# Expert layers of a small transformer moved into a third instruction stream that borrows PSUM banks

## The chip, the cores and the metric

The kernel runs on one core of a Trainium2 chip. The metric is the device time of one execution in microseconds, from runs of the whole kernel; one more execution was recorded by the hardware profiler, and all rows below are from it. Engines: TensorE (PE, with its weight loads as PEld), VectorE (DVE), ScalarE (ACT), GpSimd (POOL) and SyncE (SP), which here issues the DMAs.

## What is computed

Eight independent batch elements (batches 0 to 7 for short) of 256 tokens by 128 features pass through two layers, each with modulated layer norms (scale, shift and a gate from a small condition vector).

```python
# layer 0, attention: an indexer picks 96 keys per query (64 local ones and the best of the others)
I = einsum('bths,h->bts', relu(q_i @ k_i.T), idx_w); idx = top_k(I, 96)
scores = (q_c . k_c[idx] + q_r . key_r[idx]) * scale;  out = softmax(scores) @ v[idx] @ W_out
# layer 0, FFN: two layers of windowed attention (8 heads, window 64) and a gated GELU network
# layer 1, attention: 16 heads of size 8, full softmax over 256 tokens
# layer 1, FFN: mixture of experts, computed for all 16 experts and one shared one
score = sigmoid(h @ gate_w.T);  top 8 of 16, weights normalised, times 2.826
y = down_0(silu(gate_0(h)) * up_0(h)) + sum_e weight_e * down_e(silu(gate_e(h)) * up_e(h))
```

Everything is float32 but the gather of keys, which multiplies one-hot matrices in bf16 with keys split into three bf16 parts.

## The kernel before, in words

**Two streams.** Elements 0, 2, 4, 6 form stream 0 and elements 1, 3, 5, 7 stream 1. Each stream has its own arena in SBUF (`mem[s]`, whose parts are used again by one stage after the other) and four of the eight PSUM banks (`banks(s)`: bank 4s + i). For each engine there is a generator per stream (`tensor_stream` line 519, `scalar_stream` 1158, `vector_stream` 1544, `pool_stream` 2073, `sync_stream` 446) that issues the instructions of its four rounds and yields between steps. `turns` (line 125) interleaves the two generators of an engine by a string written out in `STEPS_IN_TURN` (line 97): each character is a number of steps, and the streams alternate. So the order of every engine is fixed in the program, and the engines meet through semaphores (`Signals`: `at(name, n)` is the value to wait for, `one(name)` the increment).

**One round of a stream:** front (transposes of the input at line 811, layer norm, projections 826 to 840, index scores 849, top-32 search on VectorE 1777 to 1785, indices written to DRAM and read back to all partitions 455 to 468, one-hot compares 1798, gather matmuls 557), sparse attention, two windowed layers (wqkv 728 and 733, scores 671, turns 616, values 687, FFN 1002 to 1018), the 16-head attention (1033 to 1101), and the experts (1109 to 1137).

**The experts before** stand at the end of each stream's round. TensorE computes the router product, the transposes of x and the gate row into bank 3 (1113 to 1116), and gate and up of the shared expert. Then for four groups of four experts: `expert_downs` of the group before (780s, matmul at 795) overwrites the banks of its own ups, `expert_gates` (matmul at 772) writes banks 0 and 1, `expert_ups` (780) waits for the last sums (1133, 1135), because it writes banks 2 and 3 again. ScalarE applies silu (1524) and scales two of the four products (1512, summed by GpSimd at 2187 and 2191). VectorE first adds the other two products (`expert_sum`, 1636) and then multiplies silu by up for the next group (2032). GpSimd adds the halves, applies the gate row and the residual (2195, 2199, 2202), and SP stores the result (490). The next round's first transpose waits for the last silu (809), its variance matmul for the last sum (819), and its second index projection for the last scaled product (838). The tiles `moe_g`, `moe_h`, `y`, `y2`, `x_res`, `gate_row`, `tmp` and `routes` lie in the stream's arena.

**Filler.** `keep_busy` (527) issues matmuls into a bank whose content nobody reads, as many as the next character of `BUSY` says (line 103 on), ahead of waits.

**Tables.** `table` (1149) loads ScalarE's function table when the next function, in the order of issue, needs another one than the last: one for Ln and Exp (line 1153), one each for Gelu and Silu (line 1155).

Of the kernel before, what the change touches and what calls it, by code (L numbers as in the profile page):

```python
# [49 lines left out]
def shape_constants():  # L50
# [47 lines left out]
    "pe": ("822112244222g26437677323236617321212244113t1a3a5841528171a455a4632a372a4522362121d672a15222846222112222424411212"  # L98
            "221212212132115142113111123125531224212523272221217272643767732323661732121224411221f1c1a2a5841528171a3611281612"
            "31225151a452a1a1612413272a45252512282824272211123212222231114211515251511122212515152525232222527266376773232366"  # L100
            "17321212245321z021218282112229482c1k1612413272a351a321818413272a452525122828232224141122121232431152515142115111"
            "2221251515252523222252726236855743234349141222231112312231a1c3c584632a371a5558425682c3c1816222352h672f1a28232624"
            "21121222121221111211211341134115351515335"),
    "act": ("d212437327322a9274312464634322162623338122m23338262536488223426223348327221b27223345522ef33321313343545523344421"
            "35a2235442182c5542a52464634322162623338142i22231382625364a22111282421132228252322a21334822332l42j433445351536233"
            "421134553233352j573212311234312464634322162623338142n2332222364f2a2322a21334d422322623334822332g321332g321134153"
            "53546233421134553233352l55321342b43564433328233334623152a2335822172322334882224162723353317h46223a2lf43423333445"
            "2334253a225"),
    "dve": ("t4o1b89645494c4369441444544652431e341441p361c41c571c442395117571744236134a1c5715412541444242412ju151335c35583523"
            "85d3m9213833434b4e44681331144321443652471d311441h3d1d41c591e4325416541a442a2521855174429311531553134123j1112z091"  # L110
            "51431c328335c365b833256411351d4d4c78341444544652431e341441v37164591444111k25218551747111645216551744293115414541"
# [181 lines left out]
def program(nc, A, out, idx_scratch, score_scratch):  # L293
    ctx = ExitStack()
    with ctx:
# [124 lines left out]
        def cols(k):  # L420
            return slice(P * k, P * k + P)
# [1867 lines left out]
```

## Time and profile before

| what | us |
|---|---|
| timed runs, median of 3 (lowest, highest) | 1416.68 (1406.8, 1420.68) |
| the profiled execution's own time | 1413.97 |
| its span, first to last instruction | 1412.1 |
| mean granted TensorE clock over the span | 0.968 |
| TensorE busy | 1221.4 |
| VectorE busy | 905.8 |
| ScalarE busy | 868.7 |
| GpSimd busy | 362.2 |

Busy time is the union of an engine's instructions. A matmul's end is modelled and matmuls are pipelined, so a busy TensorE is not TensorE at its peak. Idle time in a row is that just before the group's instructions on the same engine, with what ended it behind the arrow; "issue" means that nothing the profile shows was waited for.

### The profile page before, as it was taken

The numbers are of one execution on the slowest core, as the hardware profiler recorded it, in microseconds if no ns is written. First come the engines' busy times: TensorE is split into PE (matmuls) and PEld (weight loads), VectorE is DVE, ScalarE is ACT, GpSimd is POOL, SyncE is SP. The second block draws the span as 40 slices with busy tenths as digits, with TensorE's granted clock in tenths as the row PEclk, the third lists the DMA queues.
The fourth block names the chain that finished last, engine by engine and source line by source line (L and its number), as shares of the span: only waits on it lengthen the run. The fifth ranks groups of instructions, "written<-read, shape, count | busy, mean of one in ns | idle before, by whom it ended". The sixth has DMA issues, their size and how long they took to land.

```text
span 1412.1 us, 29992 instructions
## 1 busy us (share of the span) xinstructions
PE 1221.4 (86%) x11446; PEld 850.2 (60%) x11446; DVE 905.8 (64%) x2920; ACT 868.7 (62%) x2237; POOL 362.2 (26%) x580
## 2 busy tenths in 40 slices
PE   7879988878988988888999799788899799898787
PEld 5546555646864655565776566556677465565466
DVE  3966676553685776765376666776546767767643
ACT  3426677538652766755775477774576467776563
POOL 0710343100281132311154022231015402422103
PEclk9889999989998998999999999999999999999999
DMA  8121000000013000000011200000001210000000
GB/s 299 49 80 23 2 1 1 1 5 5 5 59 81 15 2 1 1 1 5 5 50 29 77 4 1 1 2 1 5 9 50 74 30 2 1 1 1 1 1 8
DMA packets 31791, 34.84 MB, mean 25 GB/s; under 512 B 19168, under 2 KB 23712, under 8 KB 31136
## 3 DMA queue, kind: packets, MB, share of 16 engines
q1 hardware_dynamic: 31648, 32.92, 7.8%
q8 instruction: 91, 1.49, 0.4%
q14 instruction: 52, 0.43, 0.1%
HBM read 25.46 MB, written 7.44 MB: 23 GB/s over the span
## 4 chain that ended last, share of the span: by engine, by line
PE 53%; ACT 19%; DVE 16%; issue 4%; DMA 3%; POOL 2%; SPq 1%; DVEq 0%; POOLq 0%; ACTq 0%
ACT arena L1415 5%; PE ps L795 4%; ACT arena L1164 4%; PE ps L557 4%; PE ps L780 3%; PE ps L772 3%; PE ps L728 3%; ACT arena L1468 2%; DVE small L1958 2%; PE ps L1069 2%; DMA idxb<-idx_scratch 2%; PE ps L657 2%; PE ps L530 2%; PE ps L1052 2%; PE ps L1088 2%
## 5 line engine op out<-in xcount | busy, mean ns | idle before, releaser
L1164 ACT ACTIVATE arena<-ps 128x512 f32<-128x512 f32 (+7 forms) x560 | 258.7, 485 | 235.0 <-PE ps L580 31.3
L2106 POOL TENSOR_TENSOR arena<-arena 128x512 f32<-128x512 f32 x64 | 80.9, 1275 | 310.0 <-DVE arena L1609 308.7
L1415 ACT ACTIVATE arena<-arena,small 128x128 f32<-128x128 f32 (+1 forms) x256 | 129.9, 511 | 2.2 <-DVE small L1895 1.9
L1584 DVE CUSTOM_DVE_ANT_0 arena<-ps,mask_w_bf 128x128 f32<-128x128 f32 (+1 forms) x256 | 67.6, 321 | 65.9 <-PE ps L671 65.6
L530 PE MATMUL ps<-mean_mat 128*128 128x256 bf16 x612 | 88.0, 287 | 15.3 <-ACT arena L1164 11.7
L1958 DVE TENSOR_REDUCE small<-ps 128x4 f32<-128x1024 f32 x64 | 75.5, 1219 | 29.3 <-PE ps L1052 29.0
L1362 ACT ACTIVATE arena<-arena,small 128x224 f32<-128x224 f32 (+1 forms) x128 | 56.6, 448 | 49.7 <-DVE small L1843 49.7
L1468 ACT ACTIVATE arena<-ps 128x512 f32<-128x512 f32 x128 | 66.6, 602 | 31.3 <-PE ps L1088 31.1
L530 PEld LDWEIGHTS ps<-mean_mat 128*128 128x128 bf16 x612 | 58.8, 102 | 41.5 <-issue 16.6
L2032 DVE TENSOR_TENSOR arena<-arena,ps 128x512 f32<-128x512 f32 x64 | 42.9, 686 | 60.9 <-ACT arena L1524 47.8
L1819 DVE TENSOR_TENSOR gath<-ps,rank_tab 96x512 f32<-96x512 f32 x96 | 62.4, 680 | 29.5 <-PE ps L565 15.3
L795 PEld LDWEIGHTS ps<-w_experts,arena 128*128 128x128 f32 x544 | 64.3, 191 | 26.8 <-issue 15.2
L795 PE MATMUL ps<-w_experts,arena 128*128 128x128 f32 x544 | 69.1, 279 | 12.5 <-DVE arena L2032 7.8
L557 PE MATMUL ps<-hot_ring,arena 128*96 128x512 bf16 x192 | 56.5, 438 | 25.8 <-DVE gath L1819 18.1
L1572 DVE TENSOR_TENSOR arena<-arena,small 128x512 f32<-128x512 f32 x96 | 69.3, 722 | 3.1
L728 PE MATMUL ps<-w_wqkv,arena 128*128 128x512 f32 x128 | 64.6, 643 | 2.1 <-DVE arena L1562 2.1
L2191 POOL TENSOR_TENSOR arena<-arena 128x256 f32<-128x256 f32 x32 | 24.0, 751 | 165.1 <-ACT arena L1512 163.4
L780 PE MATMUL ps<-arena,w_experts 128*128 128x256 f32 x272 | 65.5, 381 | 0.0
L616 PE MATMUL ps<-packed,arena 128*128 128x128 f32 x384 | 61.8, 284 | 4.2 <-DVE arena L1575 2.3
L772 PE MATMUL ps<-arena,w_experts 128*128 128x256 f32 x272 | 65.3, 379 | 0.0
L1512 ACT ACTIVATE arena<-ps,arena 128x128 f32<-128x128 f32 x128 | 36.7, 373 | 35.7 <-PE ps L795 35.1
L1584 DVE CUSTOM_DVE_ANT_0 arena<-ps,mask_a_bf,small 128x192 f32<-128x192 f32 (+1 forms) x128 | 41.6, 380 | 25.9 <-PE ps L603 25.5
(288 smaller groups left out, 2934.4 us busy)
## 6 DMA issues: line engine op xcount, KB each, us to landing
idxb<-idx_scratch SPq DMA_DIRECT2D x24, 512.0 KB, 5.2
score_scratch<-arena SPq DMA_DIRECT2D x96, 64.0 KB, 1.7
w_experts<-in_experts SPq DMA_DIRECT2D x3, 1088.0 KB, 17.1
w_wqkv<-in_wqkv SPq DMA_DIRECT2D x1, 1536.0 KB, 9.2
arena<-score_scratch SPq DMA_DIRECT2D x96, 16.0 KB, 2.1
arena<-in_x SPq DMA_DIRECT2D x8, 128.0 KB, 2.2
out_x<-arena SPq DMA_DIRECT2D x8, 128.0 KB, 1.8
packed<-in_packed SPq DMA_DIRECT2D x2, 503.0 KB, 4.0
```

Source lines behind the costliest of these rows:

```text
L530: mm(to, still[:, 0:P], still, start=True, stop=True)
L557: last = mm(bank[g % 2][0:GF, :], m.kv_part[i][:, 0, :], hot[n][:, part], start=(i == 0), stop=(n < 2 and i == 2))
L728: mm(bank[2 * k + j], m.sh[:, cols(k)], wqkv[:, l, 512 * j:512 * j + 512], start=True, stop=True)\
L772: last = mm(bank[j // 2][:, L * (j % 2):L * (j % 2) + L], experts[:, 0, e, :], m.hT, start=True, stop=True)
L780: last = mm(to[:, L * (j % 2):L * (j % 2) + L], experts[:, 1, e, :], m.hT, start=True, stop=True)
L795: last = mm(bank[2 + j // 2][:, 256 * (j % 2) + P * k:256 * (j % 2) + P * k + P], m.moe_h[:, L * j + P * k:L * j + P * k + P], experts[:, ...
L1164: return act.activation(dst, src, ACT.Copy)
L1415: ins = act.activation(probs, probs, ACT.Exp, bias=nb[s][:, i, h:h + 1], scale=cqs[s][:, T, hh_:hh_ + 1], accum_out=ls[s][:, i, h:h + 1])
L1468: act.activation(m.PT1[v][:, q, :, :].rearrange("p j n -> p (j n)"), bank[q], ACT.Exp, scale=SCALE_1)\
L1584: ins = dve.tensor_tensor_reduce(masked[:, h, 0:n], bank[h % 2][:, n * (h // 2):n * (h // 2) + n], mask, 1.0, least(h), ALU.add, ALU.max, ...
L1958: st.mark(dve.tensor_reduce(to, src, AX.X, ALU.max))
L2106: ins = pool.tensor_tensor(own, own, turned, ALU.add)
```

## The change

The experts leave the streams' rounds and become a third generator on each engine (`expert_tensor`, `expert_scalar`, `expert_vector`, `expert_pool`, `expert_sync`), which runs through all eight elements in order. Its tiles move to one set of their own (`LateViews`, 4096 floats per partition), shared by all elements; only `routes` is there twice. The last layer norm of a round writes `late.hT`.

It has no banks of its own: each of the 18 products of an element goes to a bank named by the string `LENT`, taken from the main streams. `Loans.borrow` waits until the last readers of the owner's content are done, and `Loans.claim`, now called in front of every first write of a main stream, waits for the return of a bank that was lent. Gates, ups and downs of a group have banks of their own; downs overwrite the ups' banks as before. TensorE's order in a group becomes gates of the next group, downs of this one, ups of the next. VectorE's products of a group come before the sums of the group before.

All turn strings are new (they now name the stream of each turn), so are the counts of filler: 612 matmuls before, 516 after, and none in front of the downs. The two waits for the output's store in the front (479, 2148) go. The DMA scratch is cut to 512.

```diff
 def turns(engine):
-    s = 0
-    for n in STEPS_IN_TURN[engine]:
-        yield from [s] * int(n, 36)
-        s = (s + 1) % NS
+    runs = STEPS_IN_TURN[engine]
+    for s, n in zip(runs[::2], runs[1::2]):
+        yield from [int(s)] * int(n, 36)
...
+class Loans:
+    def __init__(self):
+        self.emptied, self.returned = {}, {}
+    def claim(self, pe, bank, *emptied):
+        if bank in self.returned:
+            pe.wait_ge(*self.returned.pop(bank))
+        self.emptied[bank] = emptied
+    def borrow(self, pe, bank, returned):
+        for wait in self.emptied.pop(bank, ()):
+            pe.wait_ge(*wait)
+        if bank in self.returned:
+            pe.wait_ge(*self.returned.pop(bank))
+        self.returned[bank] = returned
...
+        def before_in_experts(s, r):
+            return (1 - s, r) if s else ((1 - s, r - 1) if r else None)
...
             def ln_var(n):
                 yield
+                claim([2], ("ln_rstd", n + 1))
                 keep_busy(bank[2][:, 0:L])
...
-                if r > 0:
-                    pe.wait_ge(*at("e_silu", 0))
+                claim([0], ("xT_copied", 1))
                 for k in range(NT):
                     last = pe.transpose(bank[0][:, cols(k)], m.x_tok[:, k, :], ident[:, :])
...
+        def expert_tensor(pe):
...
+                for i in range(1, 6):
+                    if i < 5:
+                        for j in range(2):
+                            yield
+                            bank = borrowed(4 * i - 2 + j, "e_silu", 2 * i + j)
+                            for h in range(2):
+                                last = mm(bank[:, L * h:L * h + L], experts[:, 0, 4 * i - 3 + 2 * j + h, :], late.hT, ...)
+                            last.then_inc(*one("e_gate"))
+                    yield
+                    pe.wait_ge(*at("e_hidden", 2 * i - 1))
+                    for j in range(1 if i == 1 else 2):
...
+                        last.then_inc(*one("e_down"))
+                    if i < 5:
+                        ups = []
+                        for j in range(2):
+                            yield
+                            name, count = ("e_sum", i + 1) if j == 0 else ("e_tmp", i)
+                            ups.append(borrowed(4 * i + j, name, count))
...
+                            last.then_inc(*one("e_up"))
...
# scalar: the copy of the next input waits until the router has read xT; in the third stream silu comes ahead of the scaling
                 act.wait_ge(*at("x_turned", 1))
+                if r > 0:
+                    act.wait_ge(*at("route_mm", 0))
                 copy(m.xT, bank[0][:, 0:L]).then_inc(*one("xT_copied"))
...
# vector, third stream
                 for i in range(1, 6):
-                    yield from expert_sum(i - 1)
                     if i < 5:
...
                             dve.wait_ge(*at("e_silu", 2 * i + j))
+                            dve.wait_ge(*at("e_down", 2 * i - 1))
                             dve.wait_ge(*at("e_up", 2 * i + j))
-                            dve.wait_ge(*at("e_down", 2 * i - 1))
...
+                    yield from expert_sum(i - 1)
...
+            streams = [tensor_stream(pe, s) for s in range(NS)] + [expert_tensor(pe)]
...
-    nc = bacc.Bacc("TRN2", target_bir_lowering=False, num_devices=1)
+    nc = bacc.Bacc("TRN2", target_bir_lowering=False, num_devices=1, dynamic_dma_scratch_size=512)
```

In the third stream an element's first writes into the shared tiles wait for the element before: `late.hT` for its last up products, silu for its last hidden product, VectorE's first hidden product for its last downs, `x_res` for its last sum, `y` for its store.

## Rows read from the trace of the kernel before

**Rows 1.** The page: span and busy time of each engine.

```profile
span 1412.1 us, 29992 instructions
...
PE 1221.4 (86%) x11446; PEld 850.2 (60%) x11446; DVE 905.8 (64%) x2920; ACT 868.7 (62%) x2237; POOL 362.2 (26%) x580
```

**Rows 2.** Groups by line: busy, mean ns of one, idle before and its releasers.

```profile
L530 PE MATMUL ps<-mean_mat 128*128 128x256 bf16 x612 | 88.0, 287 | 15.3 <-ACT arena L1164 11.7 <-DVE arena L1594 2.6 <-DVE arena L1636 1.1
L795 PE MATMUL ps<-w_experts,arena 128*128 128x128 f32 x544 | 69.1, 279 | 12.5 <-DVE arena L2032 7.8 <-DVE arena L2020 4.3
L780 PE MATMUL ps<-arena,w_experts 128*128 128x256 f32 x272 | 65.5, 381 | 0.0
L772 PE MATMUL ps<-arena,w_experts 128*128 128x256 f32 x272 | 65.3, 379 | 0.0
L795 PEld LDWEIGHTS ps<-w_experts,arena 128*128 128x128 f32 x544 | 64.3, 191 | 26.8 <-issue 15.2 <-ACT arena L1500 7.0 <-ACT arena L1524 3.9
...
L557 PE MATMUL ps<-hot_ring,arena 128*96 128x512 bf16 x192 | 56.5, 438 | 25.8 <-DVE gath L1819 18.1 <-DVE hot_ring L1798 7.0 <-ACT arena L1164 0.6
```

**Rows 3.** Line 1493, the router, in two windows: durations in ns, first and last start.

```profile
L1493 ACT ACTIVATE arena<-ps x2: 198/207/216, 327.5 to 356.1; 128x32 f32<-128x32 f32 x2
...
L1493 ACT ACTIVATE arena<-ps x2: 198/213/228, 1351.1 to 1366.2; 128x32 f32<-128x32 f32 x2
```

**Rows 4.** Line 811, first transposes of elements 2 and 3, 345 to 420 us.

```profile
L811 PE MATMUL ps<-packed,arena x4: 272/272/273, 365.8 to 394.8; 128*128 128x128 f32 x4
```

**Rows 5.** Busy time by stretch, with experts and fronts (first of three, and the sum).

```profile
core 0: us, PE busy (x) PEld busy (x) DVE busy (x) ACT busy (x) POOL busy (x), PEclk, DMA share, GB/s
327.00:480.00 153.00, 137.59 (x1381) 101.52 (x1379) 99.05 (x353) 96.64 (x245) 46.47 (x68) 0.97 0.14 38
...
sum 463.00, PE 419.62 PEld 306.58 DVE 287.90 ACT 294.45 POOL 135.44; mean PE 139.87 PEld 102.19 DVE 95.97 ACT 98.15 POOL 45.15
```

**Rows 6.** The same for the three stretches between them.

```profile
480.00:668.00 188.00, 158.43 (x1395) 103.55 (x1391) 126.17 (x363) 117.71 (x307) 44.92 (x76) 0.96 0.01 2
...
1165.00:1350.00 185.00, 158.24 (x1483) 103.90 (x1480) 123.05 (x362) 124.74 (x326) 45.14 (x76) 1.00 0.00 1
sum 560.00, PE 475.78 PEld 314.76 DVE 378.76 ACT 363.64 POOL 134.78; mean PE 158.59 PEld 104.92 DVE 126.25 ACT 121.21 POOL 44.93
```

**Rows 7.** Filler (line 530) alone in both sets of stretches: the two sums.

```profile
sum 463.00, PE 17.39; mean PE 5.80
...
sum 560.00, PE 42.66; mean PE 14.22
```

**Rows 8.** Busy time of three windows of 50 us, columns as in rows 5.

```profile
100.00:150.00 50.00, 47.93 (x789) 31.54 (x788) 32.62 (x120) 30.54 (x98) 4.39 (x5) 0.97 0.10 22
1050.00:1100.00 50.00, 46.98 (x323) 36.36 (x323) 36.44 (x140) 35.60 (x84) 22.83 (x37) 1.00 0.11 36
1350.00:1400.00 50.00, 48.27 (x307) 41.96 (x307) 25.88 (x78) 28.78 (x66) 7.78 (x11) 1.00 0.01 1
```

**Rows 9.** Filler (line 530) alone in the first two of them; the third has none.

```profile
100.00:150.00 50.00, 0.78 (x4) 0.97 0.10 22
1050.00:1100.00 50.00, 1.15 (x9) 1.00 0.11 36
```

**Rows 10.** Chain that ended last, 1350 to 1412: start, us, what.

```profile
1369.49 0.68 PE ps L795 x4
1370.18 1.73 PE ps L772 x8
...
1389.35 1.78 PE ps L795 x16
...
1401.71 0.70 DVE arena L2032
```

**Rows 11.** Groups by line: VectorE's sums, and ScalarE's loads of Gelu's and Silu's tables.

```profile
L1155 ACT ACT_TABLE_LOAD x40 | 51.3, 1283 | 0.7
...
L1636 DVE SCALAR_TENSOR_TENSOR arena<-ps,arena 128x128 f32<-128x128 f32 x128 | 39.0, 346 | 23.7 <-PE ps L795 21.8
```

**Rows 12.** Groups by line: the weight loads of the windowed values.

```profile
L687 PEld LDWEIGHTS ps<-arena 128*64 128x64 f32 x512 | 27.3, 137 | 38.9 <-issue 29.3 <-ACT arena L1164 9.5
```

More of the change, by code:

```diff
@@ L104 @@
[L104 to L108, printed above, removed]
@@ L511, in _ @@
                 sp.dma_start(dst, src).then_inc(sig("late_loaded"), 16)
-            streams = [sync_stream(sp, s) for s in range(NS)]
+            streams = [sync_stream(sp, s) for s in range(NS)] + [expert_sync(sp)]
             for s in turns("sp"):
@@ L530, in keep_busy, with claim @@
                     mm(to, still[:, 0:P], still, start=True, stop=True)
+            def claim(used, *emptied):
+                for i in used:
+                    loans.claim(pe, 4 * s + i, *(at(name, n) for name, n in emptied))
             def ln_center(n, src):
@@ L914, in tensor_stream @@
                 yield
+                claim(range(4), ("x_updated", 1))
                 keep_busy(bank[1][:, 0:L])
@@ L1041, in tensor_stream @@
                     yield
+                    claim(range(4), ("x_neg", v + 1))
                     if v == 0:
@@ L1108, in tensor_stream, with borrowed @@
                 yield from ln_var(5)
+        def expert_tensor(pe):
+            mm = pe.matmul
+            signals = [Signals(sig, s) for s in range(NS)]
+            for b in range(B):
+                s, of = b % NS, signals[b % NS]
+                of.r = b // NS
+                m, at, one = mem[s], of.at, of.one
+                def borrowed(n, name, count):
+                    loans.borrow(pe, lent(b, n), at(name, count))
+                    return ps[:, lent(b, n), :]
                 yield
-                keep_busy(bank[0][:, 0:L])
+                bank = borrowed(0, "x_res", 1)
@@ new lines, in expert_tensor @@
+                    for j in range(1 if i == 1 else 2):
+                        for h in range(1 if i == 1 else 2):
+                            e = 0 if i == 1 else 4 * i - 7 + 2 * j + h
+                            for k in range(NT):
+                                first = L * (2 * j + h) + P * k
+                                last = mm(ups[j][:, L * h + P * k:L * h + P * k + P], late.moe_h[:, first:first + P],
+                                          experts[:, 2, e, :], start=True, stop=True)
+                        last.then_inc(*one("e_down"))
@@ new lines, in expert_tensor @@
+                    if i < 5:
+                        ups = []
[3 more added lines that the diff above has]
+                            ups.append(borrowed(4 * i + j, name, count))
+                            for h in range(2):
+                                last = mm(ups[j][:, L * h:L * h + L], experts[:, 1, 4 * i - 3 + 2 * j + h, :], late.hT, start=True, stop=True)
+                            last.then_inc(*one("e_up"))
@@ L1488, in scalar_stream, with expert_scalar @@
                 yield from ln_rstd(5)
-                yield
+        def expert_scalar(act):
+            signals = [Signals(sig, s) for s in range(NS)]
+            for b in range(B):
+                s, of = b % NS, signals[b % NS]
+                of.r = b // NS
+                at, one = of.at, of.one
+                last = before_in_experts(s, of.r)
                 yield
```

369 lines of the change are left out of this document (212 added, 157 removed).

## The prediction

> **What bounds the kernel now.** I read the page's totals first [rows 1]: TensorE is busy 1221.4 of 1412.1 us, VectorE 905.8, ScalarE 868.7, GpSimd 362.2. The reader is to see one engine near its limit and three with room. The profiled execution took 1413.97 us against its span of 1412.1, 2.7 under the median of the three timed runs, 1416.68.
>
> TensorE's figure holds filler: 612 matmuls of line 530 whose output nobody reads, 88.0 us [rows 2]. So real matmul time is 1221.4 - 88.0 = 1133.4 us, 80% of the span. The rest, 278.7 us, is idle or filler, and the question is which part of it this change can reach.
>
> Then I cut the span at events that the trace places [rows 3, 4]. Batch 0 reaches its router (line 1493) at 327.5 us, but batch 2, the next one in the same arena, has its first transpose (line 811) only at 365.8, and batch 3 at 394.7 after batch 1's router at 356.1. In both streams the next batch waits for nearly the whole expert phase: its first transpose waits for the last silu (line 809). The last pair of routers comes at 1351.1 and 1366.2, three rounds later. One round of two batches is about 341 us ((1351.1 - 327.5) / 3).
>
> The tables by stretch have three stretches in which experts, the next fronts and the gathers run (327 to 480, 668 to 820, 1007 to 1165), and between them three in which only attention, FFN and the last block run. The first three sum to 463 us with TensorE busy 419.62 [rows 5]; filler in the same windows is 17.39 [rows 7]. Real work is 402.2 us, 86.9%. The other three sum to 560 us with 475.78 busy [rows 6] and 42.66 filler [rows 7]: 433.1 real, 77%. The emptier stretches are the ones that hold no expert work, and the turn strings of the changed kernel put none there: TensorE's string has passed the last expert turn of a pair by 1.25 rounds of the main streams. So the change can only refill the 463 us. Its first-order ceiling is 463 - 402.2 = 60.8 us.
>
> **The change part by part.**
>
> *Experts as a third stream.* Nothing is removed from TensorE but filler; the matmuls of lines 772, 780 and 795 return one for one (65.3 + 65.5 + 69.1 = 199.9 us in all [rows 2], 25 us a batch). What moves is when the next front may start: right after its stream's router products are written, so 327.5 instead of 365.8, some 38 us earlier in either stream. Seen as a chain the three reachable rounds could each give 38 us, which is more than TensorE can deliver; so TensorE's packing of the 463 us decides. How dense can it be? Three windows of 50 us bound it [rows 8, 9]: experts of the last pair 48.27 busy with no filler (96.5%); first-round gather and attention 47.93 - 0.78 = 94%; experts over a front 46.98 - 1.15 = 92%. I take 92%, the best that a mix of experts and a front reached: 402.2 / 0.92 = 437.2, so 25.8 us saved, some 9 a round. Low end: the share stays at 86.9%, nothing saved. High end: 96.5% gives 402.2 / 0.965 = 416.8, 46.2 saved.
>
> *The tail.* The last two batches have no front to overlap, and now share one set of work tiles, so batch 7's experts follow batch 6's. In the chain of waits of the end [rows 10] TensorE is the chain from 1369.5 to 1401.6 with no gap between expert pieces; a group of four experts costs 1.73 for gates, as much for ups of the same shape, and 1.78 for downs, 5.24 us. In the new order one group's ups (1.73) are followed by the next group's gates (1.73) and only then by its downs. The last VectorE product of a group, 0.70 us after the ups, is ready inside the gates. One batch alone therefore packs TensorE as two do now, and the end (scale by ScalarE 0.37 + 0.53, GpSimd pieces of 0.72 us) is the same. I take 0; if each of the four groups of batch 7 exposes its product once, it is 4 x 0.70 = 2.8 us; if the earlier order frees the 15.1 us between the two routers (1351.1, 1366.2) a little better, a gain of the same size.
>
> *VectorE forms the next products ahead of the last sums, and ups go to another bank.* Before, the ups of a group wait for the four sums of the last one (line 1133), 4 x 346 ns [rows 11] = 1.4 us, because they share banks 2 and 3. Now they don't. 32 groups make 44 us of latency; almost all of it lies beside the other stream's matmuls, since line 780's matmuls show 0.0 us of idle before them and line 795's 12.5 us [rows 2]. So 0 to -12.5 us; it is already inside the packing above, I add nothing.
>
> *Bank loans: added waits on TensorE.* A batch borrows 18 banks. Each borrow waits for the owner's last reader and each later claim for the loan's return: by count of the diff some 54 waits a batch in, some 20 out, 34 x 8 = 272 more. If satisfied they cost issue time. The nearest row is line 687, whose weight loads stand behind two or three waits: 29.3 us of "issue" idle over 512 loads [rows 12], 0.06 us. Upper end 272 x 0.06 = 16 us, if none hides under a running matmul; lower end 0, where the sequencer is ahead of the array, busy 86% of the span. I take 2 us. That they are not satisfied is the first rival.
>
> *ScalarE's tables.* Before there are 40 loads of Gelu's or Silu's table, 1283 ns each [rows 11], and about as many back. Silu steps are spread between the Exp and Ln steps of fronts, five silu steps a batch: at worst 5 x 8 pairs instead of the present 40 - 16 = 24 silu loads (16 are Gelu's), 16 more pairs, 41 us of ScalarE; at best fewer than now. ScalarE is busy 96.64 of 153 us in such a stretch [rows 5], so 56 us of idle hide most of it. I take 0 on the path; a load costs 1.28 where the next front's Ln waits behind it.
>
> *Filler.* The strings give 516 in place of 612, 96 x (88.0 / 612 = 0.144) = 13.8 us less of busy time in places where TensorE waits anyway: 0 on the path, up to 13.8. *Moved waits:* GpSimd's memset (line 2151) and the score read-back (line 479) no longer wait for the output's store; behind them stand small transfers of 16 KB and one memset a batch, and GpSimd is busy 26% of the span [rows 1], so I take 0. SP's queue now holds the output store as a stream of its own, and nobody waits for it but the next batch's first sum. The smaller DMA scratch moves nothing.
>
> Sum: 1414.0 - 25.8 + 2 = 1390.2. From the median of 1416.7 that would be 1392.9; I say **1391 us**.
>
> *A rule beside it.* TensorE was granted 0.97 of full speed in the first expert stretch [rows 5], which is its lower level (1.2 GHz) for some 6% of it (2 x 0.03) and 2.4 for the rest; of the stretches without experts the first had 0.96 and the last 1.00 [rows 6]. The Trainium skill (TensorE: Matmul & The Clock Gate, "HAM oscillation — how this bites in real kernels") puts the cost at half the throttled time, and says that waits between bursts cause it. By that rule denser fronts give back up to 463 x 0.06 / 2 = 14 us more, an estimate from the page's formula; the sum does without it, since part of that time is idle in which the clock costs nothing.
>
> **The rivals.**
>
> *Head-of-line waits (slower).* TensorE runs one written order. The third stream puts some 23 steps a batch, 184 in all, between steps of the main streams, and nearly all wait for ScalarE, VectorE or a loaned bank. One that comes early stops all three streams. For it: the downs' loads already wait 26.8 us and their matmuls 12.5 over 40 steps [rows 2], less 15.2 of issue 24.1 us, 0.6 us a step. Against it: gates show 0.0. At 0.14 us a step (25.8 / 184) the gain is gone; above 0.22 (25.8 + 14) it is slower by 1%. At 0.3 us a step: 55 - 26 = +29, so 1443 us.
>
> *No better packing (same).* The idle of the stretches is not lack of work but the fronts' chain: DMA of idxb, the compares, gathers; the gathers of line 557 wait 25.8 us for VectorE [rows 2]. If experts run out before these gaps, 86.9% stays: 1414 to 1417 us. That the change doesn't do what it says is the same case: loans that keep the main stream's claims waiting as long as the old order did.
>
> *Larger gain.* The fronts' start 38 us earlier and the clock's share bring 96.5%: 1414 - 46 + 2 = 1370 us. For it speaks that weight loads fill only 101.52 of 153 us [rows 5] against 41.96 of 50 in the last pair [rows 8]. [...]
>
> **How the numbers follow.** Forecast 1391 us (its own range 1378 to 1403): 0.50. Larger gain, 1370: 0.19. No better packing, 1415: 0.18. Head-of-line waits, 1443: 0.13. The bound of 1% is 14 us, about what a measurement of this kernel can tell from no change (its three runs lie 1406.8 to 1420.7). Faster by over 1%: most of the first and all of the second, 0.67. Within 1%: 0.20. Slower: 0.13. The range for 8 in 10 is 1362 to 1424: it leaves out the worst of the waits and packing beyond 96.5%.
>
> **What would show it.** First transposes (line 811) of batches 2 and 3 within some 5 us of routers 0 and 1; rounds of some 332 us between routers of one stream; TensorE's real share of the expert stretches at 92% and that between them still near 77%; the end after the last router near 43 us. Wrong if real share stays at 87%, if idle in front of the expert lines passes 50 us, if loads of Gelu's and Silu's tables exceed 55, or if the span between the stretches changes by more than 10 us: then the new order, not the third stream, made the result.

## The result and the profile after

The changed kernel takes 1403.1 us, median of 16 runs (1395.18 to 1416.66), against 1415.95 us of the kernel before, also 16 runs. The ratio is 0.9912, 95% interval 0.9889 to 0.9934: 12.8 us or 0.9% faster, where 1391 us and 1.8% were forecast. The direction was right and the gain half of the forecast. The profiled execution spans 1401.2 us against 1412.1 [rows 1].

The page of the changed kernel, span and busy time of each engine:

```profile
span 1401.2 us, 29802 instructions
...
PE 1211.0 (86%) x11350; PEld 846.4 (60%) x11350; DVE 901.3 (64%) x2920; ACT 864.8 (62%) x2231; POOL 361.8 (26%) x580
```

TensorE has 96 matmuls less, the 96 filler ones, and is busy for the same share of the span. Groups by line that answer to [rows 2] and [rows 11]; filler is line 588 now, the downs are 1219, gates 1210, ups 1229, VectorE's products 2153, its sums 2098, and the loads of Gelu's and Silu's tables 1248:

```profile
L588 PE MATMUL ps<-mean_mat 128*128 128x256 bf16 x516 | 73.0, 287 | 11.0 <-ACT arena L1257 5.1 <-DVE arena L1704 3.2 <-ACT arena L1338 2.3
L1219 PE MATMUL ps<-w_experts,late 128*128 128x128 f32 x544 | 71.5, 285 | 8.9 <-DVE late L2153 5.3 <-DVE late L2144 3.6
L1219 PEld LDWEIGHTS ps<-w_experts,late 128*128 128x128 f32 x544 | 68.2, 198 | 16.7 <-DVE late L2153 8.9 <-DVE late L2144 5.0 <-issue 1.3
L1210 PE MATMUL ps<-late,w_experts 128*128 128x256 f32 x256 | 66.1, 393 | 2.1 <-DVE small L1931 1.3 <-ACT arena L1257 0.8
L1229 PE MATMUL ps<-late,w_experts 128*128 128x256 f32 x256 | 64.0, 387 | 4.4 <-ACT late L1617 2.3 <-DVE small L1931 1.2 <-ACT arena L1411 0.9
L1248 ACT ACT_TABLE_LOAD x37 | 47.5, 1283 | 0.7
L2098 DVE SCALAR_TENSOR_TENSOR late<-ps,late 128x128 f32<-128x128 f32 x128 | 38.8, 345 | 2.0 <-PE ps L1219 0.9
```

Idle in front of the downs fell from 12.5 to 8.9 us at the matmuls and from 26.8 to 16.7 at their loads, but gates and ups, which showed 0.0, now show 2.1 and 4.4. The table loads fell from 40 to 37. And the same expert matmuls take longer: 71.5 + 66.1 + 64.0 us and 10.7 for the shared expert (lines 1201 and 1202) are 212.3, where they were 199.9 [rows 2]. Two further executions of the changed kernel give 211.9 and 211.4. The median of a gate is the same; the extra is in some of them (gates before, then gates now; duration in ns, lowest, median and highest):

```profile
L772 PE MATMUL ps<-arena,w_experts x272: 379/379/382, 327.3 to 1399.5; 128*128 128x256 f32 x136
```

```profile
L1210 PE MATMUL ps<-late,w_experts x256: 379/379/634, 327.4 to 1386.7; 128*128 128x256 f32 x128
```

The front did move. Line 853 is the first transposes of a batch (811 before, [rows 4]), line 1195 the router's matmuls; each view gives the first and the last start in its window, 300 to 400 us and, for the second router row, 1320 to 1400:

```profile
L853 PE MATMUL ps<-packed,arena x4: 272/273/273, 321.7 to 378.5; 128*128 128x128 f32 x4
L1195 PE MATMUL ps<-packed,late x8: 254/262/263, 323.9 to 380.9; 128*128 128x16 f32 x8
...
L1195 PE MATMUL ps<-packed,late x8: 254/262/263, 1328.5 to 1366.0; 128*128 128x16 f32 x8
```

Batch 2's front starts at 322 instead of 366, 2 us ahead of batch 0's router. The routers of [rows 3] are ScalarE's line; TensorE's router matmuls (line 1113 before), which compare directly with line 1195, started at 326.4 and 354.9, and at the end at 1349.7 and 1365.2. So batch 1's router comes 26 us later, at 380.6: the two streams stand 57 us apart instead of 29. Batch 6's router comes 21 us earlier, batch 7's at the same time as before within 1 us, and the end behind it takes 35 us instead of 46.

For the balance I cut both executions from stream 0's router to the end of stream 1's attention output (the products with `w_vo`, line 921 before, 970 now), so that the three stretches together hold the same work (5286 matmuls without filler before, 5273 after). First before, then after, columns as in [rows 5]; in each fence the stretches with experts:

```profile
327.00:503.00 176.00, 158.98 (x1758) 115.01 (x1758) 115.49 (x404) 111.86 (x283) 55.84 (x84) 0.97 0.12 33
668.00:856.00 188.00, 170.33 (x1869) 122.48 (x1870) 117.22 (x427) 122.05 (x311) 54.02 (x84) 0.97 0.11 31
1007.00:1187.00 180.00, 165.58 (x1835) 118.46 (x1831) 111.84 (x404) 116.79 (x292) 53.64 (x84) 0.97 0.12 32
sum 544.00, PE 494.89 PEld 355.95 DVE 344.55 ACT 350.71 POOL 163.51; mean PE 164.96 PEld 118.65 DVE 114.85 ACT 116.90 POOL 54.50
```

```profile
324.00:510.00 186.00, 167.99 (x1843) 120.52 (x1844) 119.61 (x427) 119.86 (x313) 54.77 (x84) 0.97 0.11 31
667.00:830.00 163.00, 155.45 (x1710) 112.37 (x1699) 108.41 (x384) 102.76 (x263) 47.67 (x75) 0.96 0.13 36
995.00:1168.00 173.00, 157.27 (x1777) 112.14 (x1779) 110.02 (x393) 111.69 (x283) 54.29 (x83) 1.00 0.12 34
sum 522.00, PE 480.71 PEld 345.03 DVE 338.04 ACT 334.31 POOL 156.74; mean PE 160.24 PEld 115.01 DVE 112.68 ACT 111.44 POOL 52.25
```

Filler alone in the same stretches, before and after:

```profile
sum 544.00, PE 24.71; mean PE 8.24
```

```profile
sum 522.00, PE 9.03; mean PE 3.01
```

Real work is 494.89 - 24.71 = 470.2 of 544 us before, 86.4%, and 480.71 - 9.03 = 471.7 of 522 after, 90.4%. The same work takes 22 us less. The single stretches do not hold the same work: the first has 103 matmuls more (stream 1's last block now falls into it), the second 99 and the third 17 less, so their lengths (10 us more, 25 and 7 less) say little by themselves. The real share does: 86.3 to 87.4% in the first ((158.98 - 7.15) / 176 and (167.99 - 5.51) / 186), 85.5 to 94.4% in the second, 87.6 to 89.8% in the third. The three stretches between them went from 479 to 483 us, the start from 327 to 324. Behind stream 0's last router:

```profile
1350.00:1366.00 16.00, 15.02 (x106) 11.64 (x106) 7.54 (x26) 12.43 (x23) 0.72 (x1) 1.00 0.00 1
1366.00:1412.00 46.00, 36.90 (x226) 33.27 (x224) 20.93 (x58) 18.02 (x47) 13.78 (x19) 0.96 0.02 7
```

```profile
1329.00:1366.00 37.00, 34.24 (x267) 26.87 (x267) 14.98 (x44) 27.44 (x55) 3.98 (x6) 1.00 0.00 1
1366.00:1401.00 35.00, 23.57 (x143) 20.92 (x142) 13.83 (x40) 11.72 (x29) 10.54 (x15) 0.96 0.03 8
```

62 us before, 72 after, and TensorE idle for 10.1 us of it before, for 14.2 after. So -22 + 4 - 3 + 10 = -11, the difference of the spans. But of the 10 us at the end 6 are work that now stands there, while the start holds 5.6 us less, and only 4 are new idle. To leave moved work out, take idle and filler together, and real matmul time by itself:

| us | before | changed | second execution | third |
|---|---|---|---|---|
| idle + filler, start | 80.9 | 83.5 | 80.0 | 79.2 |
| idle + filler, stretches with experts | 73.8 | 50.3 | 50.4 | 50.3 |
| idle + filler, stretches between | 113.8 | 115.0 | 114.4 | 115.1 |
| idle + filler, end | 10.1 | 14.2 | 14.1 | 14.0 |
| real matmul time | 1133.4 | 1138.0 | 1145.0 | 1142.6 |

The packing is worth 23.4 to 23.6 us in each execution. What takes it down to 11, 8 and 11 us is the end (4 us of idle) and real matmul time, which grew by 5 to 12 us, while the expert matmuls alone take 11.5 to 12.4 us more; start and the stretches between move by less than 3.

### The profile page after: what moved, and what is told of

It reads as the page before. It is cut to its first block, busy times and chain, and to the rows that moved or that the text cites. A ratio compares the mean times of both kernels' runs of the same rounds, so it can differ in the third digit from the quotient of the medians.

```text
span 1401.2 us, 29802 instructions
## 1 busy us (share of the span) xinstructions
PE 1211.0 (86%) x11350; PEld 846.4 (60%) x11350; DVE 901.3 (64%) x2920; ACT 864.8 (62%) x2231; POOL 361.8 (26%) x580
## 4 chain that ended last, share of the span: by engine, by line
PE 36%; ACT 14%; DVE 10%; POOL 4%; issue 3%; DMA 1%; SPq 1%; POOLq 0%; DVEq 0%; ACTq 0%
ACT arena L1510 4%; ACT arena L1257 3%; PE ps L1219 3%; DVE small L2046 2%; PE ps L621 2%; PE ps L1229 2%; PE ps L801 2%; PE ps L1210 2%; ACT arena L1563 2%; PE ps L1115 1%; PE ps L728 1%; PE ps L1134 1%; PE ps L588 1%; PE ps L1041 1%; PE ps L759 1%
## 5 line engine op out<-in xcount | busy, mean ns | idle before, releaser
L1257 ACT ACTIVATE arena<-ps 128x512 f32<-128x512 f32 (+5 forms) x544 | 254.9, 490 | 231.2 <-PE ps L767 26.3
L2046 DVE TENSOR_REDUCE small<-ps 128x4 f32<-128x1024 f32 x64 | 75.4, 1219 | 26.3 <-PE ps L1115 25.8
L1219 PE MATMUL ps<-w_experts,late 128*128 128x128 f32 x544 | 71.5, 285 | 8.9 <-DVE late L2153 5.3
L1219 PEld LDWEIGHTS ps<-w_experts,late 128*128 128x128 f32 x544 | 68.2, 198 | 16.7 <-DVE late L2153 8.9
L2153 DVE TENSOR_TENSOR late<-late,ps 128x512 f32<-128x512 f32 x64 | 42.9, 683 | 48.5 <-PE ps L1229 44.9
L1457 ACT ACTIVATE arena<-arena,small 128x160 f32<-128x160 f32 (+1 forms) x128 | 56.8, 447 | 24.0 <-DVE small L1931 23.9
L1210 PE MATMUL ps<-late,w_experts 128*128 128x256 f32 x256 | 66.1, 393 | 2.1 <-DVE small L1931 1.3
L1229 PE MATMUL ps<-late,w_experts 128*128 128x256 f32 x256 | 64.0, 387 | 4.4 <-ACT late L1617 2.3
L2321 POOL TENSOR_TENSOR late<-late 128x256 f32<-128x256 f32 x32 | 24.4, 762 | 156.8 <-ACT late L1631 154.9
L684 PEld LDWEIGHTS ps<-packed,arena 128*128 128x128 f32 x384 | 43.7, 143 | 25.7 <-issue 19.2
L759 PE MATMUL ps<-arena 128*64 128x128 f32 x512 | 42.6, 287 | 19.0 <-ACT arena L1257 12.0
L1694 DVE CUSTOM_DVE_ANT_0 arena<-ps,mask_a_bf,small 128x128 f32<-128x128 f32 (+1 forms) x128 | 41.6, 380 | 27.2 <-PE ps L670 27.0
## 6 DMA issues: line engine op xcount, KB each, us to landing
w_experts<-in_experts SPq DMA_DIRECT2D x3, 1088.0 KB, 15.9
```

The costliest lines, as they stand in the source:

```text
L684: last = pe.transpose(bank[2][:, cols(h)], probs[:, h, :], ident[:, :])
L1210: last = mm(bank[:, L * h:L * h + L], experts[:, 0, 4 * i - 3 + 2 * j + h, :], late.hT, start=True, stop=True)
L1219: last = mm(ups[j][:, L * h + P * k:L * h + P * k + P], late.moe_h[:, first:first + P], experts[:, 2, e, :], start=True, stop=True)
L1229: last = mm(ups[j][:, L * h:L * h + L], experts[:, 1, 4 * i - 3 + 2 * j + h, :], late.hT, start=True, stop=True)
L1257: return act.activation(dst, src, ACT.Copy)
L1694: ins = dve.tensor_tensor_reduce(masked[:, h, 0:n], bank[h % 2][:, n * (h // 2):n * (h // 2) + n], mask, 1.0, least(h), ALU.add, ALU.max, ...
```

## The experiments

All medians are of five rounds or more, each with the kernel before on the same chip. The changed kernel was run again twice as a base.

**The base.** No edit.

> The changed kernel as it stands, on the same chip as the three kernels that follow, so that they can be set against it and not only against the kernel before. Expected: ratio 0.991 to the kernel before (0.989 to 0.993), some 1403 us, expert stretches 522 us with 48 us of them neither matmul nor weight load, and an end of 35 us behind the last router.

> The changed kernel as it stands, the base for the three that follow on the same chip. Expected: 0.991 to 0.993 of the kernel before.

Measured: 1405.8 and 1403.2 us, ratios 0.9931 (0.9891 to 0.9972) and 0.9927 (0.9903 to 0.9951). As expected. In the first of these the expert stretches sum to 524 us and the end took 37.

**VectorE's order undone.**

```diff
                 for i in range(1, 6):
+                    yield from expert_sum(i - 1)
                     if i < 5:
...
-                    yield from expert_sum(i - 1)
```

> VectorE's four sums of a group come ahead of the next group's products again, as before the change; everything else, the order between the streams too, stays. Theory (the order on VectorE is part of what packs TensorE: the products of the next group are then 4 x 0.35 = 1.4 us later in each of 24 groups, half of it exposed in the expert stretches): 6 to 17 us slower than the changed kernel, and idle in front of the down products (matmuls and weight loads, 25.6 us together now) grows by as much. Rival (the forecast's zero: other streams' matmuls cover it): within 2 us. Nothing of the calculation changes.

Measured: 1421.7 us, ratio to before 1.0053 (1.0005 to 1.0100), 15.9 us above the base: slower than the kernel before. Groups by line of this kernel; the products are line 2154 here:

```profile
L1219 PE MATMUL ps<-w_experts,late 128*128 128x128 f32 x544 | 75.1, 294 | 19.2 <-DVE late L2154 15.6 <-DVE late L2144 3.6
L1219 PEld LDWEIGHTS ps<-w_experts,late 128*128 128x128 f32 x544 | 70.9, 206 | 28.6 <-DVE late L2154 21.1 <-DVE late L2144 5.0 <-issue 1.1
L1210 PE MATMUL ps<-late,w_experts 128*128 128x256 f32 x256 | 67.5, 399 | 8.5 <-ACT late L1617 5.0 <-ACT arena L1257 2.2 <-DVE small L1931 1.3
...
L2098 DVE SCALAR_TENSOR_TENSOR late<-ps,late 128x128 f32<-128x128 f32 x128 | 38.7, 344 | 23.6 <-PE ps L1219 22.8
```

The downs' matmuls wait 10.3 us more, all for the products, and the gates 6.4 more, most of it for the silus that wait for the products in turn: 16.7 us, about the loss, though over the whole span TensorE is idle only some 12.5 us more and busy 2.5 more than in the base's profile. On VectorE the idle moved to the sums (2.0 to 23.6 us): in the new order of TensorE the downs come behind the next gates, so the sums of a group can start late, and a product that stands behind them is held back though its own input is there. That last step is the reading of the code and of these waits; the run shows the waits. The stretches with experts take 187, 172 and 181 us (base 182, 161 and 181), those between are unchanged (157, 165, 161; base 159, 164, 160): the loss is in the first two, with the third as long as in this base. The theory holds, and the rival, the forecast's zero, falls. The turn strings and the loans were not rewritten for this order, so this doesn't say what a third stream with the old order would be worth if it were planned for it.

**The tail.** Batch 7's `x_res` and `gate_row` get places in a dead part of stream 1's arena, and ScalarE's copy no longer waits for GpSimd's last sum of batch 6.

```diff
-                if last is not None:
+                x_res, gate_row = (late.x_res, late.gate_row) if b < B - 1 else (own_x_res, own_gate_row)
+                if last is not None and b < B - 1:
                     act.wait_ge(*Signals(sig, last[0]).at("y_ready", 1, last[1]))
```

> Batch 7's x_res and gate_row lie in a dead part of stream 1's arena, so ScalarE's copy no longer waits for GpSimd's last sum of batch 6. In the trace of the changed kernel TensorE is idle from 1364.3 to 1372.5, and the chain there goes through that copy (1369.9) to a table load of 1.3 and a silu. Theory (the shared single set of tiles is what the tail pays): the copy starts right behind the router's softmax, 1366.5, and the end comes 3 to 5 us earlier: 0.997 of the changed kernel. Rival (the tail is bound by routing weights and GpSimd's pieces in any case, or by late.hT): 0, within 1 us.

> Batch 7's own x_res and gate_row once more, since the first comparison left the size open: its medians differed by 5.7 us, while its trace showed 3 us at the place itself (router to the first down product 5.0 us, against 7.8 to 8.2 with the shared tiles). Theory: 3 to 4 us faster than the changed kernel, all of it behind the last router. Rival (the rest of those 5.7 us was real too): 5 to 7 us faster.

Measured: 1400.2 and 1401.2 us, 5.7 and 2.0 below the bases; ratios to before 0.9899 (0.9860 to 0.9937) and 0.9910 (0.9885 to 0.9935). The comparison with the base doesn't resolve it; the mechanism is in the chains. The chain of waits of the changed kernel, start, us, what:

```profile
1364.38 1.15 ACT late L1631 x4
...
1368.88 0.73 POOL late L2332
...
1369.92 0.27 ACT late L1602
...
1370.21 1.28 ACT L1248
...
1371.50 0.39 ACT late L1608
...
1371.98 0.43 DVE late L2144
...
1372.45 0.71 PE ps L1219 x4
```

From batch 6's last scaling over five steps of GpSimd, the copy, a table load, silu and product to the first down of batch 7. TensorE is not idle all that time: batch 6's last piece ends at 1364.3, then come the router, the transposes, the shared expert and the first eight gates, with these two gaps (in brackets) around them:

```profile
1365.68 0.59 PE L1195 MATMUL ps<-packed,late 128*128 128x16 f32 x4 [1.43 <-DVE late L1665]
...
1372.45 0.71 PE L1219 MATMUL ps<-w_experts,late 128*128 128x128 f32 x4 [3.10 <-DVE late L2144]
```

With batch 7's own tiles:

```profile
1361.79 0.59 PE ps L1197 x4
...
1362.90 0.21 ACT late L1599
...
1365.11 0.64 DVE late L2131
...
1366.31 0.43 DVE late L2147
```

Now it goes through batch 7's own router and VectorE's choice of experts, and the first down starts 5.0 us after the router's first matmul, where it took 6.7:

```profile
1366.78 0.71 PE L1221 MATMUL ps<-w_experts,late 128*128 128x128 f32 x4 [1.32 <-DVE late L2147]
```

The gap in front of it is 3.1 us in all ten profiles in which batch 7 waits for batch 6's output, and 1.3 in all four with its own tiles: 1.8 us, not the theory's 3, since the expectations took the whole of 1364.3 to 1372.5 for idle. But there is a second part. The same ten microseconds behind the gap, in a second and the first execution of the changed kernel and then with batch 7's own tiles:

```profile
1370.00:1380.00 10.00, 6.90 (x29) 5.70 (x28) 3.62 (x10) 4.21 (x8) 0.89 (x2) 0.83 0.05 15
```

```profile
1370.00:1380.00 10.00, 7.55 (x45) 6.93 (x46) 2.99 (x7) 5.29 (x12) 0.25 (x1) 1.00 0.05 15
```

```profile
1363.00:1373.00 10.00, 8.68 (x50) 7.59 (x49) 5.00 (x18) 4.64 (x10) 2.46 (x4) 1.00 0.05 15
```

In the first the granted clock is down behind the gap and the ups that follow take 2.92 us instead of 1.73. Of the ten profiles with the shared tiles four have ups of 1.73 there and six of 2.68 to 3.38; all four with batch 7's own have 1.73. So the wait costs 1.8 us always and about as much again in more than half of the executions: the end behind the last router takes 33.7 us in each of the four, and 35.5 or 36.9 to 37.5 with the shared tiles. The theory is right, at a size of 2 to 3.5 us.

**What the loans' waits cost, and which bank is lent.**

```diff
-            pe.wait_ge(*self.returned.pop(bank))
+            back = self.returned.pop(bank)
+            for _ in range(2):
+                pe.wait_ge(*back)
```

(the same in `borrow`), and for the second kernel 29 of the 144 digits of `LENT` changed, with the order kept.

> Every wait of a claim or a loan stands twice in TensorE's queue, the second of the pair always satisfied at once; nothing else changes. It doubles the number of waits that the prediction priced at 0.06 us each (272 more than in the kernel before, taken as 2 us, bounds 0 to 16). Theory (the sequencer runs ahead of the array, so a satisfied wait is hidden): within 3 us of the changed kernel, 1405.8 in the last comparison. Rival (each costs its issue time): 16 us slower, and issue idle of TensorE grows by as much.

> The same order on every engine, but 29 of the 144 loans go to other banks. Theory (loaned banks come back long before they are claimed, so that which bank is lent plays no part, and all of the result lies in the order): within 3 us of the changed kernel. Rival (late returns are what keeps the expert stretches from the 92% of the forecast): a shift of 5 us or more in either direction, seen as idle in front of the main streams' first writes.

Measured: 1406.8 us, ratio to before 0.9925 (0.9900 to 0.9950), and 1407.4 us, 0.9957 (0.9928 to 0.9986). The doubled waits cost nothing that can be measured (the interval leaves room for some 3 us). Counted from the programs, they are 213 more waits on TensorE, and the page shows 29972 instructions against 29802, 170 more. The change itself added 67 waits to TensorE (1705 against 1638), not 272. The other banks may cost something, up to 6 us, but the intervals overlap (the changed kernel's is 0.9889 to 0.9934); the expert stretches of this kernel sum to 520 us, base 524. That run alone doesn't settle whether banks come back late, but the trace of the changed kernel does: matmuls of the main streams wait 0.4 us in all for a reader of a lent bank (lines 621 and 1154, for ScalarE's 1631), and gates and ups 4.2 us in all for the owner's last readers. Late returns are not what keeps the stretches from 92%.

**Filler.** None, half, a quarter, half as many again, and the old amount, by scaling the digits of `BUSY`; half also in the kernel before; half and a quarter with batch 7's own tiles.

> All 516 filler matmuls are left out (their results are read by nobody, so the calculation is whole). Theory (filler stands where TensorE waits and keeps the granted clock at 0.966): the clock falls below 0.95 and the kernel is 1 to 4% slower; the stretches that lose it are those between the expert stretches, which hold 60 of the 73 us. Rival (filler delays more than it gives, since strings put it ahead of waits that end early): faster by up to 1%, with the clock where it was.

> Half as much filler again at the same places: 774 matmuls in place of 516, 36 us more of busy TensorE. Without any filler the kernel was 7 us slower, the granted clock 0.961 against 0.969, real matmul time 32 us longer and idle as much shorter. Theory (what is left of low clock falls in the first 50 us and in single dips that filler doesn't reach, while each further filler matmul delays what stands behind it): clock unchanged at 0.97, 2 to 10 us slower than the changed kernel. Rival (the trend of the last run goes on, and the 96 filler matmuls that the change took away were missed): clock 0.98 or above and 2 to 5 us faster.

> 258 of the 516 filler matmuls, about half at each place. None cost 7 us and half as many again cost 15. Theory (near its best amount, filler's two effects, delay and clock, cancel): within 4 us of the changed kernel, clock 0.965. Rival (delay is linear, so half the filler saves half of what more filler cost per matmul, 258 x 15/258 = 15 us, and the clock is lost only with the last of it): 5 to 10 us faster.

> Both of the above: batch 7's own x_res and gate_row, and 258 filler matmuls. If the two are independent, its ratio is the product of theirs, 0.997 x (0.997 to 1.003) of the changed kernel by the theories, down to 0.99 by the rivals; the best version so far if half the filler is no loss.

> 129 filler matmuls and batch 7's own x_res and gate_row. With 258 and the same residual it was 1392.4. Theory (the clock's loss of the run without any, 7 us slower than 516, comes gradually): 2 to 8 us slower than with 258, clock 0.962 to 0.965. Rival (the loss hangs on the last few places): equal or up to 3 us faster.

> The changed kernel with the old amount of filler, 612, spread over its 516 places by one factor. Half as many again cost 15 to 18 us for 258, so 0.06 to 0.07 us each. Theory (part of the change's gain is the 96 filler matmuls that it left out): 3 to 7 us slower than the changed kernel, ratio to before 0.995 to 0.998. Rival (only the packing counts): within 2 us of it, ratio 0.991 to 0.993.

> The kernel before, with 307 of its 612 filler matmuls. Theory (the amount of filler is a matter of its own, which the forecast took at zero on the path: each filler matmul there costs what it costs in the changed kernel, 6.2 us for 258, so 0.024 us each): 6 to 9 us faster than the kernel before, ratio 0.994 to 0.996. Rival (filler delays only the dense order of the third stream; in the old order it stood in gaps): within 2 us, or slower by what the clock loses.

The last column is the mean granted clock over the kernel's timed runs, not that of the one profiled execution.

| kernel | filler | us | ratio to before, 95% interval | clock |
|---|---|---|---|---|
| changed | 516 | 1403.1 | 0.9912 (0.9889 to 0.9934) | 0.968 |
| changed, none | 0 | 1412.8 | 0.9975 (0.9929 to 1.0021) | 0.956 |
| changed, half | 258 | 1397.0 | 0.9874 (0.9846 to 0.9901) | 0.968 |
| changed, old amount | 612 | 1402.3 | 0.9894 (0.9861 to 0.9927) | 0.967 |
| changed, half as many again | 774 | 1420.9 | 1.0037 (1.0004 to 1.0069) | 0.960 |
| half, batch 7's own tiles | 258 | 1392.4 | 0.9853 (0.9819 to 0.9887) | 0.967 |
| a quarter, batch 7's own tiles | 129 | 1393.9 | 0.9858 (0.9826 to 0.9891) | 0.969 |
| before, half | 307 | 1422.8 | 1.0044 (1.0022 to 1.0065) | 0.957 |

The old amount in the new order costs nothing (0.9894), so the 96 filler matmuls left out are no part of the gain that can be measured; the theory there fell. Half of it in the old order makes the kernel before 0.44% slower, also against the theory, and here the clock goes with it: 0.957 over 12 runs, 0.964 over the 17 of the kernel before beside them. In the new order the same halving leaves the clock at 0.968 (base 0.967) and is 6.2 us faster than its base. Where, the windows show: in the half_filler kernel stream 0's router comes at 322 and 660 us, so its first round is 338 us long where the base took 344, and the later rounds are as long as the base's (326 and 336 against 325 and 336). The first expert stretch of this kernel, and the filler in it:

```profile
322.00:503.00 181.00, 163.91 (x1824) 117.35 (x1823) 117.95 (x427) 118.78 (x309) 55.28 (x84) 0.98 0.11 32
...
322.00:503.00 181.00, 2.80 (x14) 0.98 0.11 32
```

In the three executions of the changed kernel it took 186, 182 and 185 us, with 5.5 us of filler (31 matmuls) in the first. So this stretch got 1 to 5 us shorter for 2.7 us of filler, and the router ahead of it comes 2 us earlier; that filler in this stretch delays it fits, but no run takes it out there alone. Without any filler this round is shorter still (335 us), but the last one takes 347, where three executions of the changed kernel have 334 to 341; the clock column of its stretch between experts reads 0.92:

```profile
1164.00:1331.00 167.00, 133.42 (x950) 88.03 (x946) 109.52 (x323) 105.67 (x278) 37.17 (x62) 0.92 0.00 1
```

No run shifts the experts' order against that of the main streams. So what holds stream 1's last block back at 328 to 381 us, and what a better order of the first round would give, stays open.

The best version is the changed kernel with half the filler and batch 7's own tiles: 1392.4 us, 1.5% under the kernel before and 0.8% under the changed one (1403.2 in the same comparison).

## Why the prediction was half right

**The packing.** "I take 92%" gave 25.8 us. Measured over equal work: 86.4 to 90.4%, 22 us, or 23.5 counted as idle and filler. The mechanism is as predicted (the front of batch 2 starts 44 us earlier, and the same work fills less time), and the term was 2 to 4 us too large: 92% was the best window of 50 us, taken as the mean of all. The average hides a difference: two stretches reached 94.4 and 89.8%, and the first stayed at 87.4% with stream 1's last block pushed into it, though I had priced all three alike, "some 9 a round". That the term came so close is in part luck: the forecast's windows (463 us) end earlier than those measured here (544 us), and over these 92% would have been 33 us (544 - 470.2 / 0.92).

**The matmuls.** This step failed: "the matmuls of lines 772, 780 and 795 return one for one (65.3 + 65.5 + 69.1 = 199.9 us in all". They return in number, but take 211.4 to 212.3 us in three executions, and real matmul time as a whole, held at 1133.4 us, is 1138.0 to 1145.0: a term of 5 to 12 us that the sum has at nothing. The mean clock was no lower (0.966, 0.969 and 0.972 against 0.968). At the end, where experts stand alone, the 64 gates of a pair take 15.5 us (line 1210), in the three stretches with fronts 16.4 to 17.5. Why they take longer there no run tests.

**The tail.** "I take 0" failed too: TensorE is idle behind stream 0's last router for 14.0 to 14.2 us instead of 10.1. I looked only at TensorE's order within one batch. The text of the change says that `x_res` waits for the last sum of the element before; for batches 0 to 6 that sum is long done, for batch 7 it is on the path and costs 2 to 3.5 us. The other 6 us by which this stretch grew are work of the lagging stream: stream 1's router now comes 56 us behind stream 0's in the first three rounds (28 to 43 before) and 37 instead of 15 us behind it in the last, while stream 0's three rounds got 19 us shorter together (1328.5 - 323.9 against 1349.7 - 326.4). The start holds 5.6 us less of work for it, so this is no loss by itself.

**Together** they explain the size. Forecast: -25.8 + 2 = -23.8. Measured in the first execution: -23.5 for the packing, 0 for the waits, +4.1 for the end, +4.6 for longer matmuls, and +3.8 in start and the stretches between (-0.2 and -0.5 in the other two executions, where the matmuls took 11.6 and 9.2 more): -11.0. There is one profile of the kernel before, so a few us of this are that execution's own.

**VectorE's order** stood as "0 to -12.5 us; it is already inside the packing above, I add nothing". It is inside the packing, but not small: without it the third stream, in the order as written, is 0.5% slower than before, and 15.9 us slower than its base. The forecast looked at the old bank conflict (ups waiting for sums, 1.4 us a group) and not at what the new TensorE order does to the sums: with gates ahead of downs the sums come later, and so does what stands behind them on VectorE. The zero cost the sum nothing, since the order was right in the kernel; but the largest difference between two runs here hangs on a step that I had booked as nothing.

**Bank loans.** Taken as 2 us, measured within the noise of 0 for 213 more waits; at the 0.06 us each that I read from line 687 they would have cost 13. My count of 272 was too high: the change added 67. The idle of 29.3 us of "issue" at the old line 687 [rows 12] is therefore not to be read as the price of satisfied waits.

**Tables.** At worst 16 more than the 40 were forecast, taken as 0 on the path; they went down to 37, as the zero needed.

**Filler.** "0 on the path, up to 13.8": 612 in the new order measured the same as 516, so the zero was right for the change, though half the filler helps and half as many again costs some 15 to 18 us.

**Head-of-line waits.** Idle in front of the expert matmuls is 8.9 + 2.1 + 4.4 = 15.4 us, 3 more than before and far from the 50 that would have made me wrong (I should have said that matmuls were meant: with the weight loads, which run beside matmuls, it is over 50 both before and after). It became 32.2 us (19.2 + 8.5 + 4.5) when VectorE's order was undone. The rival was real; the order of one engine kept it away.

**The clock.** It stayed where it was: 0.963 and 0.967 over the runs of the two bases, 0.965 and 0.964 over those of the kernel before beside them. So denser fronts gave nothing back that can be seen. The size of such a dip can be read from two executions of the changed kernel, third expert stretch: the first is printed above (995 to 1168, clock 1.00, 173 us), the other is

```profile
989.00:1170.00 181.00, 165.17 (x1777) 116.38 (x1778) 110.74 (x393) 111.34 (x284) 54.35 (x83) 0.94 0.12 32
```

181 us at 0.94. The Trainium skill (TensorE: Matmul & The Clock Gate, "HAM oscillation — how this bites in real kernels") puts the cost at half the time at the lower level: 181 x 0.12 / 2 = 10.9 us, an estimate by that rule. Measured were 8, so the trace agrees in size. Such dips come at other places in each execution: the first expert stretch had 0.97 where the third had 1.00, and 1.00 where the third had 0.94.

**What I named beforehand.** First transposes within 5 us of the routers: 2 us ahead of either. Rounds of 332 us: 344, 328 and 334 in stream 0. Share 92%: 90.4; between the expert stretches near 77%: 76.2. End of 43 us after the last router: 35, shorter because batch 6 was already done.

## What to carry to other kernels

When work is made a stream of its own, look at the order on every engine that serves it, not only on the bound one: here gates ahead of downs made the sums late, and two exchanged steps on VectorE decided between 0.9% faster and 0.5% slower. Balance each round and the tail by themselves, count idle apart from work that only moved, and don't hold the busy time of the moved matmuls fixed. Tiles shared by all elements can cost nothing until the last one. Filler tuned for a looser order is worth scaling again after the order gets denser, with the mean clock of many runs beside each amount.

## What the runs showed of the hardware

A wait that is already satisfied cost TensorE nothing visible: 213 more of them (170 more instructions on the page) moved 1405.8 us (the changed kernel on another chip) to 1406.8, while the kernel before gave 1414.3 and 1414.6 beside them.

In front of the last batch's downs TensorE was idle for 3.1 us, behind 3.7 us of work and 1.4 us of idle before that. The granted clock was down behind it in six of ten profiled executions (the next eight ups took 2.68 to 3.38 us) and not in the other four (1.73). With 1.3 us idle at the same place it was down in none of four.

One kernel's time goes with the clock it is granted. Over the 16 runs of the changed kernel the mean clock lay between 0.959 (1416.7 us) and 0.976 (1397.7), and a line through them gives some 8 us for 0.01; over 27 runs of the kernel before it is 7.3. A profile is one draw from this.

Filler holds some clock, but not in proportion to its amount. Without any the runs had 0.956 (0.947 to 0.968) against 0.963 of the base on the same chip, and by that line the difference (0.0077) is some 6 us of the 7 that were lost; in the one profiled execution real matmuls took 1176.8 us where the base had 1145.0. Halved in the kernel before, 0.957 against 0.964. In the new order a quarter, half, all and the old amount have 0.967 to 0.969 on their chips, the base's further runs 0.963 and 0.967, and half as many again 0.960 against 0.965 of the kernel before: more filler did not raise it. Why a quarter of it does as well as all stays open.
